# Moving the input transposes, the next projection and the additions of y inside the pair loop of a two-layer kernel

## The reference

```python
h = _layernorm(x) * (1 + ca) + sa
x = x + ga * _L0_attn_ref(h, ...)   # xp = h @ Wp + bp; scan over the tokens; @ C @ Wo + bo; + h; layer norm
h = _layernorm(x) * (1 + cb) + sb
x = x + gb * _L0_ffn_ref(h, ...)    # silu(h@w1)*(h@w2), gelu(@h1), gelu(@h2), @w3: 128 -> 512 -> 512 -> 512 -> 128
...                                 # layer 1: gated linear attention, then a feed-forward part with routed low-rank experts
```

## Time and profile before

| what | us |
|---|---|
| median of 3 runs | 516.63 (516.24 to 518.31) |
| the profiled execution | 518.73, of which the span of the trace is 516.9 |
| front, by TensorE's timeline | about 0 to 241 |
| end of pair 0, 1, 2: start of `y(i, 0)` | 83.57, 135.66, 184.24 |

### The profile page before, as it was taken

The page is one execution under the profiler, slowest core; times in us unless marked ns, Lnnn a source line. Parts: engine busy times, 40 slices in busy tenths (PEclk is TensorE's granted clock), DMA queues, the critical chain, the costliest instruction groups (busy, mean ns, idle before and its releaser), DMA issues.

```text
span 516.9 us, 11888 instructions
## 1 busy us (share of the span) xinstructions
PE 485.2 (94%) x4560; PEld 387.3 (75%) x4560; DVE 348.3 (67%) x1009; ACT 341.4 (66%) x648; POOL 170.4 (33%) x244
## 2 busy tenths in 40 slices
PE   8679999999999999998997999999999898999995
PEld 5657876787678777876775787777777687888874
DVE  6787886879686968373674877768767573544433
ACT  3969868775877578955673676766757555555640
POOL 2420541034102201210434356374463815433311
PEclk8879999999999999999998999999999999999998
DMA  8600000000000300000332221322213000001001
GB/s 278 220 1 2 2 0 1 0 3 0 1 1 2 141 1 1 1 1 21 102 81 91 74 66 59 103 62 80 80 45 102 21 3 0 22 22 40 22 21 42
DMA packets 24250, 23.44 MB, mean 45 GB/s; under 512 B 3808, under 2 KB 22944, under 8 KB 24064
## 3 DMA queue, kind: packets, MB, share of 16 engines
q1 hardware_dynamic: 23136, 22.12, 14.3%
q10 hardware_dynamic: 1056, 0.52, 0.4%
HBM read 20.27 MB, written 2.36 MB: 44 GB/s over the span
## 4 chain that ended last, share of the span: by engine, by line
PE 44%; ACT 3%; issue 3%; POOL 2%; DVE 1%; POOLq 0%
PE bank L2094 6%; PE bank L170 6%; PE bank L172 5%; PE bank L171 5%; PE bank L2008 5%; PE bank L2059 3%; PE bank L2033 3%; PE bank L2048 3%; PE bank L2021 2%; PE bank L246 2%; PE bank L2086 1%; ACT att_qT L1827 1%; PE bank L2102 1%; ACT h_hi L252 1%; PE bank L2075 1%
## 5 line engine op out<-in xcount | busy, mean ns | idle before, releaser
L1119 PE MATMUL bank<-ffn_g_hi,w_hi 128*128 128x512 f32 x288 | 116.9, 406 | 0.1
L1120 PE MATMUL bank<-ffn_g_lo,w_hi 128*128 128x512 f32 x288 | 114.1, 396 | 0.0
L654 DVE TENSOR_TENSOR ffn_g_lo<-ffn_full,ffn_g_hi 128x512 fp32r<-128x512 f32 x96 | 67.1, 699 | 27.3 <-ACT ffn_full L902 26.0
L1119 PEld LDWEIGHTS bank<-ffn_g_hi,w_hi 128*128 128x128 f32 x288 | 54.3, 188 | 14.0 <-issue 1.9
L1120 PEld LDWEIGHTS bank<-ffn_g_lo,w_hi 128*128 128x128 f32 x288 | 54.3, 189 | 11.6
L902 ACT ACTIVATE ffn_full<-bank,cols 128x512 f32<-128x512 f32 x64 | 44.3, 697 | 21.5 <-PE bank L1120 16.5
L1665 POOL TENSOR_TENSOR att_vw<-att_v,att_prob 128x128 f32<-128x128 f32 x64 | 25.2, 418 | 85.3 <-DVE att_prob L1477 85.3
L1854 ACT COPY att_qT<-bank 128x512 f32<-128x512 f32 x64 | 37.1, 589 | 12.2 <-PE bank L172 8.0
L1477 DVE TENSOR_TENSOR_SCAN att_prob<-att_prob,bank 128x512 f32<-128x512 f32 x32 | 37.4, 1205 | 7.7 <-DMA att_prob<-cut_rows 7.7
L1488 DVE TENSOR_TENSOR att_prob<-bank,att_prob 128x512 f32<-128x512 f32 x32 | 21.9, 690 | 25.2 <-PE bank L2008 24.2
L756 POOL TENSOR_TENSOR ssm_out_rstd<-ssm_out_var,neg_half 128x4 f32<-128x4 f32 x8 | 9.2, 1154 | 82.2 <-DVE ssm_out_var L535 82.1
(11 more groups left out here) (231 smaller groups left out, 1159.9 us busy)
## 6 DMA issues: line engine op xcount, KB each, us to landing
att_prob<-cut_rows SPq DMA_DIRECT2D x64, 128.0 KB, 3.1
att_wide<-cum_rows SPq DMA_DIRECT2D x64, 56.0 KB
out<-att_vw SPq DMA_DIRECT2D x7, 256.0 KB, 2.3
x<-in_x SPq DMA_DIRECT2D x3, 512.0 KB, 12.3
w_raw<-in_w_all SPq DMA_DIRECT2D x1, 1152.0 KB, 9.9
w_raw<-in_w_all SPq DMA_DIRECT2D x1, 768.0 KB, 10.8
x<-in_x ACTq DMA_DIRECT2D x2, 256.0 KB, 3.5
w_raw<-in_w_all SPq DMA_DIRECT2D x1, 512.0 KB
```

Of the source, the lines that this page charges most:

```text
L654: dve.tensor_tensor(lo, full[j % 4][:, :], hi.bitcast(F32), ALU.subtract).then_inc(low, 1)
L1119: pe.matmul(acc, w[0], x[0], start=start, stop=False)
L1120: return pe.matmul(acc, w[0], x[1], start=False, stop=stop)
```

## The change

Five things move; no instruction is added or taken away.

1. `flip_h` of the second sequence of the pair after next is issued behind body 22 in place of 21 (pairs 0 and 1).
2. `project` of pair p (p = 2, 3) is issued behind body 1 of pair p - 1, no longer behind body 23 of pair p - 2 (so it stands in the first phases of pairs 1 and 2); `bring_u` moves with it from body 1 to 2, and `scan` from body 3 to 4.
3. The two `add`s of the previous pair's y move on VectorE from bodies 4 and 7 to the end of the pair, behind `lower` of bodies 22 and 23 (pairs 1 and 2), and in pair 3 to bodies 8 and 9, ahead of `moments_att`.
4. `z` of pairs 1 and 2 is written to banks 6 and 7 in place of 4 and 5.
5. With that, what follows `yflip` in bank 4 is `y(i, 0)` in pairs 1 and 2.

```diff
@@ loop_uses
+                    if i in (1, 2) and j == 1:
+                        uses.append((("u", i + 1), 6))
                     if i < 3 and j in (8, 9):
-                        uses.append((("z", 2 * i + 2 + j - 8), 4 + j - 8))
+                        uses.append((("z", 2 * i + 2 + j - 8), 6 + j - 8 if i else 4 + j - 8))
...
-                    if i < 2 and j == 21:
+                    if i < 2 and j == 22:
                         uses.append((("flip", 2 * i + 5), 7))
-                    if i < 2 and j == 23:
-                        uses.append((("u", i + 2), 6))
@@ VectorE, layer0(i)
-                            if j == 3 and i < 3:
+                            if j == 4 and i < 3:
                                 scan(i + 1)
-                            if j in (4, 7):
-                                add(2 * (i - 1) + (j == 7))
@@ VectorE, bodies 8 to 23
                             if j in (20, 21):
                                 low_h(e + j - 20)
+                            if i and j in (22, 23):
+                                add(2 * i - 24 + j)
...
                         if i == 3:
                             if j in (8, 9):
+                                add(j - 4)
                                 moments_att(j - 8)
@@ ScalarE, layer0(i)
-                            if j == 1 and i < 3:
+                            if j == 2 and i < 3:
                                 bring_u(i + 1)
@@ TensorE
+                            if i in (1, 2) and j == 1:
+                                project(claim, i + 1)
...
-                            if i < 2 and j == 21:
+                            if i < 2 and j == 22:
                                 flip_h(claim, e + 3)
-                            if i < 2 and j == 23:
-                                project(claim, i + 2)
```

## The result

The changed kernel is slower: 523.73 us (median of 6, 521.86 to 526.99) against 516.43 (6 runs, 515.52 to 518.31), a ratio of 1.0141 with a 95% interval of 1.0109 to 1.0172, so +7.3 us, 5.6 to 8.9. The forecast was +3.75 with a range up to 522.8: the sign was right, the size half of the measured one. The profiled execution of the changed kernel took 522.15 us, its span is 520.3.

A forecast was written before the change was run, and what follows sets the result against it. TensorE, busy for 94% of the span, was taken to bound the kernel. Terms of -1.2, +2.15, +0.5 and +2.3 sum to +3.75 us on the median 516.63, so 520.4 us; own range 519.2 to 521.6, 8-in-10 range 518.0 to 522.8.

The forecast's parts named there:

- Pair 1 to body 7: Pair 0's end and pair 1's first phase: the up product of body 7 comes 1.2 us earlier.
- Only its two pauses for PE can go, 0.52 ... and 0.85: ScalarE after `normalise`: only pauses ahead of gelu(23) and `bring_y` can go, moving silu(0) from 86.33 to 84.96.
- Pair 1's end: y of sequence 2 waits for its `add` to free bank 4: PE idle 4.0 us, y 1.0 late.
- Pair 2 to body 7: Up to the up product of body 7: +2.15 us, from 1.0 bank wait, 0.95 projection, 0.2 scan against `add`.
- Pair 2's end: y of sequence 4 waits for the `add` of sequence 2 and starts 0.86 us late.
- Keys: Pair 3: keys(0) waits in bank 4 for an `add` now behind lower(8), PE idle 2.3 us more.
- the term forecast at 0.5: Pair 2's end and pair 3's first phase: up product of body 7 0.5 us later, bounds -0.2 and +0.86.
- PE runs dense to the end of front and gives nothing back: Behind the keys in pair 3: TensorE has no slack there, so the delay stays to the end of front.
- The likeliest case: The forecast itself, whole kernel: +3.75 us, 520.4 us, chance 0.62.
- The rival: The clock falls in pair 1's wait of 4.0 us ahead of y: +2.1 us more, 522.5 us, chance 0.16.
- The short keys' wait: Rival, pair 3: part of the keys' 2.3 us isn't added; 518.8 us with a third left, 518.1 with none; chance 0.14.
- The additions hold nothing: Rival, pairs 1 to 3: `add` is done before PE claims bank 4; -2.3 us in all, 514.3 us, chance 0.08.

The follow-up runs named there:

- e1: Changed kernel with both long waits of TensorE filled by matmuls of ones, 18 ahead of y of sequence 2 and 10 ahead of keys(0): ratio 1.0080, +4.1 us.
- e3: Changed kernel with the additions of sequences 4 and 5 back at bodies 4 and 7 of pair 3: ratio 1.0065, +3.4 us against the kernel before.
- e9: The changed kernel itself measured and profiled again: ratio 1.0139, +7.2 us against the kernel before.
- e10: Changed kernel with only the wait ahead of the keys filled, by 10 matmuls of ones: ratio 1.0085, +4.4 us against the kernel before.
- e2: Changed kernel with only the wait ahead of y of sequence 2 filled, by 18 matmuls of ones: ratio 1.0082, +4.2 us against the kernel before.
- e4: Kernel before with only the additions moved and z on banks 6 and 7, flips and projection as before: ratio 1.0049, +2.5 us.
- e6: Changed kernel with the additions of pairs 1 and 2 at bodies 8 and 11, those of pair 3 at 4 and 7: ratio 0.9938, -3.2 us.
- e7: Kernel before with only the two flips moved from body 21 to 22: ratio 0.9978, -1.1 us.
- e8: Kernel before with only the projection moved to body 1, and with it bring_u and the scan: ratio 1.0035, +1.8 us.
- e11: e6 with the scan of pairs 1 and 2 moved on from body 4 to 6: ratio 0.9928, -3.7 us against the kernel before.

## Why the prediction was right and wrong

*The sum, -1.2 + 2.15 + 0.5 + 2.3 = +3.75, is what the waits cost.* With the clock held (e1) the loop is +3.6. That the two agree to 0.1 is in part luck: one term was off by -0.4 and another by +0.3. The terms, from the start of the loop:

- Pair 1 to body 7: forecast -1.2, measured (92.80 - 31.24) - (96.03 - 32.84) = -1.6. The step that ran short is "Only its two pauses for PE can go, 0.52 ... and 0.85": there was a third on ScalarE. gelu(21) and gelu(22) stand merged in one row of the timeline, 1.51 long before and 1.25 after, and the quarter of a microsecond between them was also a wait for PE. silu(0) came 1.8 earlier, not 1.37, and 0.2 of that I can't place.
- Pair 1's end: y of sequence 2 forecast 1.0 late against its pair, measured (133.52 - 31.24) - (135.66 - 32.84) = -0.5 in all, so 1.1 behind the -1.6. The idle time was forecast as 4.0 and is 3.87.
- Pair 2 to body 7: forecast +2.15 from y's wait, projection and scan. In e1, where the clock holds, body 7 of pair 2 lies 115.8 behind the loop's start against 115.3 before, and that of pair 1 61.5 against 63.2: +2.2. In the changed kernel it is (148.74 - 31.24) - (148.12 - 32.84) + 1.6 = +3.8, the clock's 1.6 on top.
- Pair 2's end: y 0.9 late, forecast 0.86. Keys: (204.89 - 31.24) - (201.22 - 32.84) = +5.3, less the 2.2 at pair 2's body 7, so +3.05 where 0.5 + 2.3 were forecast. The idle time is 2.27 of that; the other 0.8 is the term forecast at 0.5. It took y's 0.9 to shrink to 0.5 on the way to body 7, and hardly any of it did: e3, without the keys' wait, is +0.85 behind `flip_ffn(6)`.
- Behind the keys "PE runs dense to the end of front and gives nothing back" held (in e1 +3.56 at keys(0), +3.64 at the loop's end), but at the lower clock +5.3 became +6.9.

*The failed step is the clock.* The likeliest case took TensorE's pace behind the waits from rows at full clock, so it put the clock at nothing. I priced the fall at +2.1 with a chance of 0.16, for the one wait ahead of y, and said that "a wait of 2.3 or 3.0 would likely be harmless", which left the keys out. The runs showed the fall at the 3.9 us in all four profiles where they were left unfilled (changed, e3, e9, e10), at 1.7 us in three and 2.3 in e10, and behind the keys' 2.3 us in two of four (changed and e9, not e2 and e4), at 1.6. The rival had its mechanism right and its price for y about right; it lacked the second place, and its chance was far too small. The waits with the clock held and the two falls, +3.6 + 1.7 + 1.6 = +6.9, are the measured loop.

The rows that should have moved the chance were at hand. Of the two gaps that I weighed, 1.8 and 4.8 us, the forecast gap of 4.0 lay nearer the one with the fall. And I overlooked a third, which is in the same list as rows 2, between its two lines: in layer 1 of the kernel before, PE stands idle for 3.7 us, and the clock is at the lower level right behind it (waits of PE over the whole span; busy by stretch):

```profile
PE bank L2033 <- issue: 3.7, 1, 3.7
...
274.00:277.50 3.50, 0.00 (x0) 0.00 (x0) 3.23 (x7) 0.45 (x1) 1.62 (x5) 1.00 0.13 41
277.50:281.00 3.50, 3.45 (x14) 2.71 (x14) 0.83 (x7) 1.35 (x3) 3.34 (x5) 0.53 0.40 119
```

*The short keys' wait* is refuted: it measured 2.27 for 2.3 (e3 shows its worth). *The additions hold nothing* is refuted for this order, but e6 comes close to that case, with the additions done long before the bank is claimed: -3.2 against the -2.3 that the rival worked out.

## What to carry to other kernels

When a reader of a buffer is moved later in its engine's list, look up who claims the buffer next: the cost is not on the engine that was relieved but on the one that claims. Making the claimant early in the same edit turns a short hold into a long idle stretch, and on TensorE that can cost twice, first the wait and then the lower clock behind it. Price a new TensorE gap with the clock behind the nearest gap in length, look for that gap in the whole trace and not only in the part that changes, and take the fall as the likely case when that one shows it.

## What the runs showed of the hardware that was not expected

TensorE's clock fell to 1.2 GHz behind an idle stretch of only 2.3 us, at the keys, in two of four executions. Both of these are the changed kernel, where the clock had fallen at y too, some 70 us earlier; whether that has to do with it is not shown. The stall in layer 1 ahead of L2033, which no experiment touches, gives more cases: it measures 2.0 to 3.7 us in the 13 profiles, and the clock fell in it, or within about 1.1 us behind it, in all three that have 3.3 us or more (before, e7, e8) and in five of the ten that have 2.0 to 3.1, the shortest being e2's 2.0. Idle stretches of 0.8, 1.0, 1.3 and 1.8 us inside the loop left it full in every profile.

The clock did not fall at the same moment each time. At y, in the changed kernel, it fell as PE resumed after 3.87 us, in e3 about 0.7 us and in e9 about 1.1 us later, and in e10 already 2 us into the wait, so that the same wait cost 1.7 us in three executions and 2.3 in another. "TensorE: Matmul & The Clock Gate" in the Trainium skill (section "Part 1: The HAM clock gate (the "warmup" mystery)") says of the rise of the clock that the number of matmuls that run ahead of it differs from run to run of one kernel. The profiles agree on the rise: ahead of the loop it comes between 0.9 us before the first transposes (before) and 2.1 us behind them (e11). That the fall moves as well is what these profiles add.

Falls that come in some executions and not in others are a likely part of the spread of one kernel's runs: the changed kernel's run from 521.9 to 527.0 us, with mean granted clocks of 0.980 to 0.969, and e1's, whose loop has no fall in the profile, from 517.8 to 525.1 with 0.988 to 0.976. Which falls these were is not shown, since only one execution of each was profiled.

Matmuls of ones into an unused bank kept the clock up at no cost that can be measured: the loop of e1 is +3.6 us, where the forecast for the waits alone was +3.75. Filling a wait so is only second best, though: e6, which removes it, is 7 us faster than e1.
